# Attention and FFN layer in one kernel: values kept in SBUF, queries and keys projected from float32r halves, first maxima two halves at a time

## The chip, the cores and the metric

The kernel runs on one core of a Trainium2 chip. The metric is device time in microseconds of one execution, given as the median of several. The engines are TensorE (PE in the profile, its weight loads PEld), VectorE (DVE), ScalarE (ACT), GpSimd (POOL) and SyncE (SP), whose queue issues most DMAs. A name with a q behind it (SPq, ACTq) is an engine's sequencer.

## What is computed

One transformer layer on x of shape 8 x 1024 x 256, all in float32, for which the reference does

```python
q, k, v = (split_heads(x @ w.T * s + b) for each of q, k, v)     # 16 heads of 16
attn = softmax(q @ k.T / 4)                                      # 1024 x 1024 per head
x = layernorm(x + ((attn @ v) @ w_o.T * s_o + b_o))
gate, up = fp4(x) @ fp4(w_gate).T, fp4(x) @ fp4(w_up).T          # width 704, fp4 by blocks of 16
x = layernorm(x + fp4(silu(gate) * up) @ fp4(w_down).T)
```

The weights of q, k, v and o are whole multiples of 8 (0 and plus or minus 8).

## The kernel before

The program has three stages, each written as five programs (one for each engine) whose order is the order of the Python text. Nothing is reordered by a planner; the engines meet at semaphores.

**Stage 1, `project`** takes the 8192 tokens in 16 chunks of 512 (`C`). For a chunk, `transpose_x` (L397) turns x into PSUM banks 0 and 1, ACT copies it to `xT` (L466), and PE computes queries and keys (L437: four blocks `m` of 128 rows, each two float32 matmuls of 512 columns) and values (L447: four token tiles `j`, each two float32 matmuls of 256 columns). A float32 matmul stands in the trace as two records. ACT reads each block of queries or keys twice, as float32 (`qf`, L479) and rounded to float32r (`parts`, L482); DVE subtracts the one from the other (L517), so that a number is kept as the sum of two float32r halves. DVE also scales the values into `vaug` (L527), where a head takes 32 columns (`AV`), 16 of values and a one. SP stores the halves in `qk_dram` (L349) and the values in `v_dram` (L356).

From chunk 4 on (`MAX_FROM`) the row maxima of the first group of heads are taken beside this. `max_tile` (L416) makes the scores of 128 queries of one head with all 1024 keys, in two banks, and `take_max` (L503) reduces them to one maximum. There are 32 (`MU`) of these for a group of four heads, three to a chunk. PE may not write the two banks again before DVE has read them (`max_read`).

**Stage 2, `attend`** runs over 32 groups (8 batches x 4 groups of four heads). A group has 16 steps `s`, each of two half steps. In a half step PE computes two score tiles of the next step (L729) and, beside them in the other half of the array's rows, the two banks of one maximum of the group after (L709); then four matmuls, one for each head, which multiply 256 columns of the exponentials with `vs` (L757, eight records, 32 output rows per head, so the four stand side by side in the array). DVE reduces the maxima (L860), ACT takes the exponentials (L813). Maxima run four steps ahead (`AHEAD`): so the stage begins with steps 12 to 15 of a group -1, which hold eight maxima of group 1 and, at the end, the first scores of group 0. `load_stacks` (L580 to L591) loads queries, keys and values of group i + 2 into one of three slots (`RING`), at the start of group i. POOL meanwhile quantizes the FFN weights.

**Stage 3, `feed`**, runs over 64 tiles of 128 tokens and ends the kernel.

## Time and profile before

| | us |
|---|---|
| median of 3 runs | 2152.37 |
| lowest, highest | 2149.47, 2155.92 |
| the profiled execution | 2149.2 |
| span of its profile | 2147.0 |
| stage 1 (0 to 235), PE busy | 217 |
| stage 2 (235 to 1552), PE busy | 1288 |
| stage 3 (1552 to 2147), PE busy | 573 |

Times in rows are from the start of the span. PE busy is the union of matmul records, whose ends are modelled. "PEclk" is the TensorE clock that was granted, as a share of 2.4 GHz: 1.00 is 2.4 GHz and 0.50 is 1.2 GHz.

### The profile page before, as it was taken

What the parts mean: (1) busy time and instruction counts of PE and PEld (TensorE: products, weight loads), DVE (VectorE), ACT (ScalarE), POOL (GpSimd) and SP (SyncE); (2) the same over time, 40 slices, a digit from 0 to 9 for tenths busy, and PEclk for the clock granted to TensorE, in tenths of its full rate; (3) what the DMA queues carried; (4) which work ended last, traced back from release to release, by engine and by line L of the source; (5) the groups of instructions that cost most, each with busy time, mean ns of one, the idle gap of its engine ahead of it and who ended that gap; (6) DMA issues with size and microseconds to landing.
All of it is one profiled execution on the core that took longest, in us unless ns stands there. A gap on an engine that the chain in (4) does not pass through costs nothing.

```text
span 2147.0 us, 41870 instructions
## 1 busy us (share of the span) xinstructions
PE 2077.8 (97%) x15708; PEld 1062.5 (49%) x15708; DVE 1885.9 (88%) x2477; ACT 1658.9 (77%) x3230; POOL 800.2 (37%) x711
## 2 busy tenths in 40 slices
PE   7999999999999999999999999999979999999998
PEld 4455433333333333333333333333457777777776
DVE  3455799999999999999999999999079999999996
ACT  4445588888888888888888888888857777777775
POOL 3000399999200000000000000000058888888885
PEclk9999899999999999999999999999999999999999
DMA  7988833533533443443453353351121211111100
GB/s 234 300 265 244 238 57 57 89 59 52 91 62 52 78 75 52 73 76 56 68 79 57 64 85 56 56 82 27 46 76 58 63 60 60 62 60 60 60 31 21
DMA packets 171985, 184.48 MB, mean 86 GB/s; under 512 B 23622, under 2 KB 134598, under 8 KB 171782
## 3 DMA queue, kind: packets, MB, share of 16 engines
q1 hardware_dynamic: 164102, 174.19, 36.5%
q10 hardware_dynamic: 7392, 7.34, 1.1%
q8 instruction: 124, 2.03, 0.4%
q14 instruction: 79, 0.65, 0.1%
q0 software_dynamic: 288, 0.27, 0.1%
HBM read 104.14 MB, written 76.02 MB: 84 GB/s over the span
## 4 chain that ended last, share of the span: by engine, by line
PE 83%; DVE 10%; ACT 3%; DMA 2%; issue 1%; POOL 1%; SPq 0%; POOLq 0%; DVEq 0%; ACTq 0%
PE ps L709 25%; PE ps L757 24%; PE ps L1010 11%; DVE negmax L860 9%; PE ps L1032 8%; PE ps L437 5%; PE ps L999 2%; PE ps L447 2%; PE ps L1021 2%; ACT craw L821 2%; PE ps L729 2%; PE ps L1040 1%; PE ps L416 1%; DMA wgu<-in_L_ffn_w_up_dram 1%; PE ps L397 0%
## 5 line engine op out<-in xcount | busy, mean ns | idle before, releaser
L860 DVE TENSOR_REDUCE negmax<-ps 128x1 f32<-128x1024 f32 x992 | 1203.8, 1221 | 38.2 <-PE ps L709 28.4
L813 ACT ACTIVATE room<-ps 128x512 f32<-128x512 f32 x2048 | 1104.9, 598 | 168.0 <-PE ps L729 132.2
L729 PE MATMUL ps<-qs,ks 50*128 50x512 f32 x2048 | 754.6, 448 | 0.5 <-ACT room L813 0.5
L709 PE MATMUL ps<-ks,qs 48*128 48x512 f32 x1984 | 726.4, 446 | 19.4 <-DVE negmax L860 18.3
L757 PE MATMUL ps<-room,vs 128*32 128x256 f32 x8192 | 655.3, 392 | 9.3 <-ACT craw L821 0.2
L709 PEld LDWEIGHTS ps<-ks,qs 48*128 48x128 f32 x1984 | 293.8, 186 | 424.2 <-DVE negmax L860 316.0
L1255 POOL TENSOR_TENSOR ctxT<-cin 128x256 f32<-128x256 f32 x64 | 58.6, 915 | 996.7 <-DMA cin<-rden 996.7
L757 PEld LDWEIGHTS ps<-room,vs 128*32 128x32 f32 x8192 | 163.5, 108 | 376.7 <-issue 214.1
L729 PEld LDWEIGHTS ps<-qs,ks 50*128 50x128 f32 x2048 | 308.0, 185 | 17.3 <-ACT room L813 14.8
L1010 PE MATMUL ps<-wguT,xqT 128*128 128x512 f32 (+1 forms) x1152 | 264.9, 383 | 2.1 <-DVE xqT L1183 2.1
L1010 PEld LDWEIGHTS ps<-wguT,xqT 128*128 128x128 f32 x1152 | 209.2, 189 | 58.4 <-issue 20.2
L1032 PE MATMUL ps<-wdT,hT 128*128 128x256 f32 (+1 forms) x768 | 191.8, 392 | 3.9 <-ACT hT L1086 3.9
L1032 PEld LDWEIGHTS ps<-wdT,hT 128*128 128x128 f32 (+1 forms) x768 | 142.0, 192 | 43.7 <-issue 26.6
L899 POOL TENSOR_SCALAR fq<-fq 88x1024 f32<-88x1024 f32 (+1 forms) x42 | 137.4, 3271 | 3.6
L437 PE MATMUL ps<-xT,wT 128*128 128x512 f32 x256 | 123.0, 619 | 2.5 <-ACT parts L482 2.5
L1057 ACT ACTIVATE centre<-mv 128x1 f32<-128x1 f32 x128 | 25.6, 200 | 112.8 <-POOL rstd L1244 112.8
L1278 POOL TENSOR_TENSOR hg<-room,hm 128x704 f32<-128x704 f32 x64 | 97.4, 1522 | 9.4 <-DVE room L1164 8.4
L517 DVE TENSOR_TENSOR parts<-qf,parts 128x512 fp32r<-128x512 f32 x64 | 43.6, 687 | 56.4 <-ACT parts L482 56.4
L893 POOL TENSOR_TENSOR fq<-wgu,rcp_w 88x1024 f32<-88x1024 f32 x4 | 7.7, 1934 | 226.6 <-DMA v_ones<-vaug 226.3
L1283 POOL TENSOR_TENSOR hq<-hg,hs 128x704 f32<-128x704 f32 x64 | 88.7, 1386 | 5.5 <-PE ps L1021 0.5
L479 ACT ACTIVATE qf<-ps,b_col,s_all 128x512 f32<-128x512 f32 x64 | 49.7, 777 | 52.8 <-PE ps L437 46.1
L1157 DVE SCALAR_TENSOR_TENSOR room<-room,hs 128x704 f32<-128x704 f32 x64 | 86.8, 1355 | 0.1
(102 smaller groups left out, 2091.9 us busy)
## 6 DMA issues: line engine op xcount, KB each, us to landing
qk_parts<-parts SPq DMA_DIRECT2D x64, 512.0 KB, 5.1
qs<-qk_parts SPq DMA_DIRECT2D x192, 128.0 KB, 4.4
ks<-qk_parts SPq DMA_DIRECT2D x192, 128.0 KB, 7.1
v_ones<-vaug SPq DMA_DIRECT2D x64, 256.0 KB, 5.7
vs<-v_ones SPq DMA_DIRECT2D x32, 512.0 KB, 9.4
ctx_raw<-craw SPq DMA_DIRECT2D x64, 256.0 KB
cin<-ctx_raw SPq DMA_DIRECT2D x64, 128.0 KB
cin<-rden SPq DMA_DIRECT2D x64, 128.0 KB
```

Source lines behind the costliest of these rows:

```text
L437: last = nc.tensor.matmul(ps[:, QK + m % 2, :], wT[:, m // 2, c, (m % 2) * P:(m % 2 + 1) * P], xT[:, i.slot(2), c, :], start=c == 0, stop= ...
L709: return nc.tensor.matmul(ps[:, MX + 2 * (item[i.k, u] % 2) + bank, :], qs[rows, i.slot(RING), pair, t * P:(t + 1) * P], ks[rows, i.slot(R ...
L729: nc.tensor.matmul(ps[:, score_bank(i, s * GH + n), :], ks[rows, slot, pair, kt * P:(kt + 1) * P], qs[rows, slot, pair, qh * BANK:(qh + 1) ...
L757: last = nc.tensor.matmul(ps[h * AV:(h + 1) * AV, PV, cols], vs[:, i.slot(RING), kt, h * AV:(h + 1) * AV], prob[:, prob_slot(i, s), h, col ...
L813: nc.scalar.activation(prob[:, prob_slot(i, s), SCORE_ORDER[n], :], ps[:, score_bank(i, s * GH + n), :], ACT.Exp, scale=float(D) ** -0.5). ...
L860: nc.vector.tensor_reduce(negmax[:, j.slot(RING), max_column(u):max_column(u) + 1], ps[:, bank:bank + 2, :], AX.XY, ALU.max, negate=True). ...
L899: link(nc.gpsimd.tensor_scalar(dst, norm, mid * mid, gain, ALU.is_gt, ALU.mult))
L1010: last = nc.tensor.matmul(ps[:, GU + n0 // BANK, 0:n1 - n0], xqT[:, a, c, :], wguT[:, b, c, n0:n1], start=n == 0 and c == 0, stop=n == len ...
L1032: last = nc.tensor.matmul(ps[:, DN, 0:H], hT[0:rows, c, :], wdT[0:rows, c, :], start=c == 0, stop=c == IC - 1)
L1157: return nc.vector.scalar_tensor_tensor(out=by(self.norm), in0=by(self.src), scalar=NUDGE, in1=self.blocks[:, 2].unsqueeze(2).to_broadcast ...
L1278: nc.gpsimd.tensor_tensor(hg[:, :], hn[:, t.slot(2)], hm[:, t.slot(2)], ALU.subtract).then_inc(sems["hgrid_ready"], 1)
L1283: nc.gpsimd.tensor_tensor(hq[:, :].rearrange("p (n e) -> p n e", e=BLK), hg[:, :].rearrange("p (n e) -> p n e", e=BLK), hs[:, t.slot(2), 1 ...
```

## The change

**Stage 1.** Values stay in SBUF, in `vals` (64 token tiles x 16 heads x 17 columns, `DV` = 16 values and a one); `v_dram`, its 64 stores and the 32 loads into `vs` are gone. ACT copies x twice, as `xT` and rounded to float32r as `xh`; DVE makes the rest `xl` = xT - xh. Queries and keys are three products of halves (`PRODUCTS`), six float32r matmuls of 512 columns for each block instead of two float32 ones. The number of `qf` buffers goes from four to two. Maxima are taken in units of 128 queries of two heads, in the two halves of the array's rows, with 512 keys, four units to a chunk; a reduce gives two half maxima, which one `tensor_tensor` (`whole_max`) joins. Chunks 4 to 11 take the first group, chunks 12 and 13 the first eight units (`LEAD`) of group 1, so stage 2 begins at step 15 of group -1. At chunk 12 (`TURN`) the whole maxima of group 0 are formed and transposed. The scales of the FFN weights are computed in chunks 2, 3 and 14 from copies loaded into `stage`, no longer ahead of chunk 0; x of chunk 0 is loaded ahead of three of the four weights.

```diff
-        load_chunk(sp, At(None, 0, 2))
-        load_chunk(sp, At(None, 1, 2))
-        sp.wait_ge(qk_consts_in, 64)
-        for j in range(2):
-            sp.dma_start(wgu[:, j], ffn_ws[j]...).then_inc(ffn_w_in[j], 16)
-        sp.dma_start(wd[:, :, :], ffn_ws[2]...).then_inc(ffn_w_in[2], 16)
+        load_weights(0)
+        load_chunk(sp, At(None, 0, 2))
+        load_weights(1)
+        load_weights(2)
+        load_chunk(sp, At(None, 1, 2))
+        load_weights(3)
...
+        def queries_and_keys(i, m):
+            wait(pe, qk_float, i.lin(4, m - 1))
+            for n, (a, b) in enumerate(PRODUCTS):
+                if m == 0:
+                    pe.wait_ge(x_split if b else xh_ready, i.lin(1, 1))
+                x_half = xl if b else xh
+                for c in range(HC):
+                    last = nc.tensor.matmul(ps[:, QK + m % 2, :], wqk[:, a, m // 2, c, (m % 2) * P:(m % 2 + 1) * P],
+                                            x_half[:, i.slot(2), c, :], ...)
...
             wait(act, v_psum, i.lin(2, -2))
+            nc.scalar.activation(xh[:, i.slot(2)], ps[:, 0:2, :], ACT.Copy).then_inc(xh_ready, 1)
             nc.scalar.activation(xT[:, i.slot(2)], ps[:, 0:2, :], ACT.Copy).then_inc(xT_ready, 1)
...
-                wait(act, qk_split, i.lin(4, m - 3))
+                wait(act, qk_split, i.lin(4, m - 1))
...
         for i in chunks():
+            if i.plus(1).ok(NCH):
+                split_x(i.plus(1))
+            if i.k == TURN:
+                whole_max(0, S // P, MU)
+                maxima_out.split(nc, dve, ps[:, MX], At(None, 0, RING), first_maxima)
+            split_qk(i, 0)
+            take_max(i, 0)
+            split_qk(i, 1)
+            values(i, 0)
+            take_max(i, 1)
+            split_qk(i, 2)
+            take_max(i, 2)
+            split_qk(i, 3)
+            values(i, 1)
+            take_max(i, 3)
+            weight_scales(scale_job(i))
```

**Stage 2.** The values' matmuls read 17 columns of `vals` for a head and write 17 rows of PSUM, still from row 32 h on. The FFN weights are loaded here, ahead of the stacks of group 2.

```diff
-                last = nc.tensor.matmul(ps[h * AV:(h + 1) * AV, PV, cols],
-                                        vs[:, i.slot(RING), kt, h * AV:(h + 1) * AV],
+                last = nc.tensor.matmul(ps[h * AV:h * AV + DV, PV, cols],
+                                        vals[:, i.k // NG * KT + kt, i.k % NG * GH + h, :],
...
-            for s in range(ST - AHEAD if i.k < 0 else 0, ST):
+            for s in range(ST - 1 if i.k < 0 else 0, ST):
...
     def sync(sp):
-        pass_1_stored(sp)
+        projections_done(sp)
+        for j in range(2):
+            sp.dma_start(wgu[:, j], ffn_ws[j]...).then_inc(ffn_w_in[j], 16)
+        sp.dma_start(wd[:, :, :], ffn_ws[2]...).then_inc(ffn_w_in[2], 16)
```

Stage 3 does the same work; its buffers, and the memory of `cin`, `xin3`, `wguT` and `wdT`, now lie where `vals` lies, and SP has one more wait (`pv_done` of group 28) ahead of the first loads of the last stage.

On PE a chunk with maxima stood so before (`xT`, `xin` are x, `ps` is PSUM):

```order
L397 MATMUL ps<-ident,xin 128x128 x8
L437 MATMUL ps<-xT,wT 128x512 x2
L416 MATMUL ps<-ks,qs 128x512 x2
L437 MATMUL ps<-xT,wT 128x512 x4
L416 MATMUL ps<-ks,qs 128x512 x2
L437 MATMUL ps<-xT,wT 128x512 x2
L447 MATMUL ps<-wT,xT 128x256 x4
L416 MATMUL ps<-ks,qs 128x512 x2
L447 MATMUL ps<-wT,xT 128x256 x4
```

and the first half of one stands so now (the `qs` read by L478 is where `xh` lies, L465 are the maxima, L488 the values):

```order
L437 MATMUL ps<-ident,xin 128x128 x8
L478 MATMUL ps<-qs,wqk 128x512 x2
L478 MATMUL ps<-xl,wqk 128x512 x2
L478 MATMUL ps<-qs,wqk 128x512 x2
L465 MATMUL ps<-ks,qs 128x512 x2
L488 MATMUL ps<-wT,xT 128x256 x2
L478 MATMUL ps<-qs,wqk 128x512 x2
L478 MATMUL ps<-xl,wqk 128x512 x2
L478 MATMUL ps<-qs,wqk 128x512 x2
L488 MATMUL ps<-wT,xT 128x256 x2
L465 MATMUL ps<-ks,qs 128x512 x2
```

Three visits to the maxima have become four, and values and queries alternate. On PE the end of stage 1 and the start of stage 2 stood so before:

```order
L447 MATMUL ps<-wT,xT 128x256 x8
L709 MATMUL ps<-ks,qs 128x512 x13
L729 MATMUL ps<-qs,ks 128x512
L709 MATMUL ps<-ks,qs 128x512
L729 MATMUL ps<-qs,ks 128x512
L709 MATMUL ps<-ks,qs 128x512
```

and stand so now:

```order
L488 MATMUL ps<-wT,xT 128x256 x2
L835 MATMUL ps<-qs,ks 128x512 x4
L815 MATMUL ps<-ks,qs 128x512
L835 MATMUL ps<-qs,ks 128x512
L815 MATMUL ps<-ks,qs 128x512
L835 MATMUL ps<-qs,ks 128x512
```

The sixteen matmuls of eight maxima (L709) ahead of and beside the first scores (L729) are gone; four scores (L835) stand alone, and then the steps of group 0 begin. On SP, stage 2 begins now with

```order
L392 DMA qk_parts<-parts 128x2x512 [waits qk_split] x8
L765 DMA wgu<-in_L_ffn_w_gate_dram 88x8x256 [waits v_ready,qk_stored1,qk_stored0]
L765 DMA wgu<-in_L_ffn_w_up_dram 88x8x256
L766 DMA wd<-in_L_ffn_w_down_dram 128x2x704
L691 DMA qs<-qk_parts 16x2x1024 x6
L691 DMA ks<-qk_parts 16x2x1024 x6
```

so three loads of 704 KB stand in the queue ahead of the twelve of group 2.

## Rows read from the trace of the kernel before

**Rows 1.** Windows: us, busy us (instructions) of each engine, PEclk, DMA share, GB/s.

```profile
0.00:235.00 235.00, 216.91 (x721) 122.07 (x721) 116.09 (x171) 112.39 (x149) 19.72 (x21) 0.98 0.89 270
249.00:1552.00 1303.00, 1277.31 (x12223) 482.06 (x12215) 1217.98 (x1075) 1130.91 (x2102) 292.53 (x118) 1.00 0.38 65
239.00:256.00 17.00, 16.34 (x70) 6.04 (x68) 13.54 (x12) 8.71 (x16) 8.56 (x4) 0.50 0.91 206
```

**Rows 2.** Chain of waits through one chunk: start us, us, what.

```profile
100.76 0.87 PE ps L397 x8
101.64 1.72 PE ps L437 x4
103.36 0.66 PE ps L416 x2
...
108.31 1.91 PE ps L437 x4
110.22 1.73 PE ps L447 x8
```

**Rows 3.** Chain of waits at the start, before chunk 1.

```profile
12.71 12.96 DMA wgu<-in_L_ffn_w_up_dram
...
31.59 0.64 DVE parts L517
```

**Rows 4.** Timeline: the wait for group 0's stacks at chunk 4.

```profile
73.19 1.22 PE L416 MATMUL ps<-ks,qs 48*128 48x512 f32 x2 [5.27 <-DMA vs<-v_ones]
74.34 5.78 PE L437 MATMUL ps<-xT,wT 128*128 128x512 f32 x8
```

**Rows 5.** Groups by line, 87 to 222 us: busy us, mean ns, idle before.

```profile
L503 DVE TENSOR_REDUCE negmax<-ps 128x1 f32<-128x1024 f32 x29 | 35.5, 1225 | 27.7 <-PE ps L416 27.7
L479 ACT ACTIVATE qf<-ps,b_col,s_all 128x512 f32<-128x512 f32 x40 | 31.1, 777 | 28.4 <-PE ps L437 28.4
...
L517 DVE TENSOR_TENSOR parts<-qf,parts 128x512 fp32r<-128x512 f32 x40 | 27.5, 687 | 31.4 <-ACT parts L482 31.4
...
L527 DVE SCALAR_TENSOR_TENSOR vaug<-ps,s_all,b_row 128x256 f32<-128x256 f32 x39 | 16.2, 478 | 0.0
...
L466 ACT ACTIVATE xT<-ps 128x1024 f32<-128x1024 f32 x10 | 10.2, 1023 | 41.2 <-PE ps L397 41.2
```

**Rows 6.** DMA issues of the start: KB each, median us to landing.

```profile
xin<-in_L_attn_x_dram SPq DMA_DIRECT2D x2, 512.0 KB, 10.0
```

**Rows 7.** Timeline from stage 1 into stage 2: start us, us, instruction, [idle before].

```profile
235.52 0.74 PE L709 MATMUL ps<-ks,qs 48*128 48x512 f32 x4 [1.17 <-DVE vaug L527]
...
238.53 2.37 DVE L860 TENSOR_REDUCE negmax<-ps 128x1 f32<-128x1024 f32 x2
...
248.56 1.08 PE L757 MATMUL ps<-room,vs 128*32 128x256 f32 x8
...
256.71 0.64 PE L757 MATMUL ps<-room,vs 128*32 128x256 f32 x8
```

**Rows 8.** Timeline of PE in the middle of stage 2.

```profile
1000.24 0.49 PE L709 MATMUL ps<-ks,qs 48*128 48x512 f32 x1
...
1000.90 0.64 PE L757 MATMUL ps<-room,vs 128*32 128x256 f32 x8
...
1001.47 0.49 PE L709 MATMUL ps<-ks,qs 48*128 48x512 f32 x1
```

**Rows 9.** Groups by form, 257 to 1552 us, weight loads: mean ns.

```profile
L709 PEld LDWEIGHTS ps<-ks,qs 48*128 48x128 f32 x1954 | 287.6, 184 | 411.7 <-DVE negmax L860 308.3 <-issue 103.4
L757 PEld LDWEIGHTS ps<-room,vs 128*32 128x32 f32 x8152 | 162.6, 107 | 373.8 <-issue 211.8 <-ACT room L813 161.3
```

**Rows 10.** Chain of waits in stage 3: float32r matmuls of 512 and 384 columns.

```profile
1709.88 4.06 PE ps L1010 x18
```

**Rows 11.** Chain of waits, half steps at the two levels of the clock.

```profile
255.11 1.01 PE ps L757 x8
...
256.78 0.57 PE ps L757 x8
```

More of the change, by code:

```diff
@@ L240, in build @@
+        third = feed(nc, sb, sem, room, buffers, x_tok, ctx_dram, rden_dram, out_tok, ps, ident, wT, s_all, b_row,
+                     wguT, wdT, wt_ready, wt_split, numbers, sums, craw_stored, rden_ready, rden_stored, cin, xin,
+                     c_in, x_in)
         with nc.Block() as block:
@@ L308, in max_tiles, with unit_at, scale_job, staged @@
         first = (i.k - MAX_FROM) * MAX_PER
-        return range(first, min(first + MAX_PER, MU))
+        return range(first, min(first + MAX_PER, MU + LEAD))
+    def unit_at(u):
+        group, n = divmod(u, MU)
+        return group, n // (2 * GP), (n // 2) % GP, n % 2
+    def scale_job(i):
+        return {MAX_FROM - 2: 0, MAX_FROM - 1: 1, NCH - 2: 2}.get(i.k)
+    def staged(job):
+        if job == 2:
+            return stage[:, 0:HC * I]
+        return stage[0:I // 8, :]
     def chunks():
@@ L421, in tensor, with values @@
+        def values(i, j):
+            if j % 2 == 0:
+                wait(pe, v_ready, i.lin(2, j // 2 - 1))
+            for c in range(HC):
+                last = nc.tensor.matmul(ps[:, VV + j // 2, (j % 2) * H:(j % 2 + 1) * H],
+                                        xT[:, i.slot(2), c, j * P:(j + 1) * P], wT[:, 0, c, :],
+                                        start=c == 0, stop=c == HC - 1)
+            if j % 2 == 1:
+                last.then_inc(v_psum, 1)
         for i in chunks():
@@ new lines, in take_max, with whole_max @@
+                nc.vector.tensor_reduce(both[:, :, pair * (S // P) + t:pair * (S // P) + t + 1], ps[:, MX:MX + 2, :],
+                                        AX.X, ALU.max, negate=True).then_inc(max_read, 1)
+        def whole_max(group, tiles, done):
+            whole, first, second = (a.rearrange("p (h t) -> p h t", t=S // P)[:, :, 0:tiles]
+                                    for a in (negmax[:, group], halfmax[:, group, 0], halfmax[:, group, 1]))
+            dve.wait_ge(max_read, done)
+            nc.vector.tensor_tensor(whole, first, second, ALU.min).then_inc(max_whole, 1)
@@ L642, in items @@
         for g in range(1, NGR):
[L643 removed]
+            for u in range(LEAD if g == 1 else 0, MU):
                 yield g, u
```

364 lines of the change are left out of this document (199 added, 165 removed).

## The prediction

> **What bounds the kernel now.** I read the windows by stage first [rows 1]. Stage 1 takes 235 us with PE busy for 217 of them and DMA at 0.89; stage 2 takes the most, PE busy 98% of it, DVE 93%. The chain of waits says which of these ends last. In a chunk of stage 1 it runs through PE alone, piece on piece [rows 2]: 0.87 for the transposes, 1.72 for four records of queries or keys, 0.66 for a visit to the maxima. A visit also makes the next four records 1.91 instead of 1.72, so it costs 0.66 + 0.19 = 0.85. A chunk is 0.87 + 4 x 1.72 + 2 x 1.73 + 3 x 0.85 = 13.8 us with maxima and 11.2 without. DVE is idle 27.7 us behind PE's maxima and 31.4 behind ACT [rows 5], so it has room here.
>
> In stage 2 the reader is to see that DVE is not the bound, though it is 93% busy. A half step is 1.23 us, from one L709 to the next [rows 8], and no idle time stands before the second on PE. Two reduces back to back take 2.37 [rows 7], so one every 1.14. PE is full: float32r matmuls for 0.66, values for 0.57 [rows 8, 11]. Whatever shortens PE's half step counts 1024 times, until about 1.14.
>
> **The change, part by part.** The sum is made against the profiled execution, 2149.2 us, which is 3.2 below the median.
>
> (1) The start of stage 1. Before, DVE waited for the FFN weights and computed their scales, and its first subtraction came at 31.59 [rows 3]. That goes. What is late next is the last of the 2 MB of w and x: its second x chunk landed about 10 us after issue at 2.7 [rows 6], and as much is loaded now. With the transposes of w_o and the copy behind it (about 1.5), chunk 0 begins at 14.5.
>
> (2) A chunk on PE. Transposes 0.87. Queries and keys: 24 float32r matmuls of 512 columns. Eighteen of the same form, 8448 columns, took 4.06 [rows 10], so one of 512 takes 0.246 and 24 take 5.9, where 16 records took 6.9. The bounds are the columns alone at 2.4 GHz (0.213, 5.1) and the 0.33 of one in a visit, where its weight load is not hidden [rows 2] (7.9). I take 5.9, the nearest form. Values stay at 3.46. A visit still has two matmuls, but in different rows of the array, as L709 and L729 have in stage 2, where they start together; 0.21 of columns goes from 0.85, so 0.64 (bounds 0.43 and 0.85). A chunk without maxima is 10.2 and one with four visits 12.8.
>
> The Trainium skill ("TensorEngine Tiling (Array Packing)", Key Properties) says that a change of tiling mode, not of tile, drains the array. By that the two halves share one drain, and the visit is 0.64; if a change of tile drained too, it would be 0.85, 40 times, 8.4 us more.
>
> (3) ACT and DVE in a chunk. ACT gets a second copy of 1.02 and has eight of 0.78, about 8 us with its DMA issue: still under PE. DVE has four reduces (4.6 at 1.14 each; two outputs instead of one, same input, so I keep 1.14 and allow 1.3), four subtractions 2.5, values 1.7 and the new subtraction on 1024 columns, about twice 0.69 less its fixed part, 1.2 (bounds 0.69 and 1.37). That is 10, beside 12.8 on PE [rows 5, 7]. But there is one pair of banks for the maxima, so PE waits where a reduce is late. Walking one chunk through the order of the three engines: the copies end 3.3 after the chunk's start, the new subtraction at 4.5, the first reduce starts at 5.5 and ends at 6.7, while PE is at the second unit at 6.25. Such waits come to 0.9. So 13.7 for a chunk with maxima.
>
> (4) Single waits in stage 1. Group 0's stacks are loaded in chunk 2 and wanted in chunk 4, as before; then PE waited 5.3 us [rows 4]. Chunk 3 is 1 us shorter now, the thirteenth load (vs) is gone: I take 4.4, between 0 and 7. Behind that wait PE ran at half pace, L416 1.22 for two [rows 4] instead of 0.66 and the eight records of L437 after it 5.8 instead of 3.6; the same loss again, 2.7. At chunk 12 the whole maxima wait behind x of chunk 13 on DVE (transposes, two copies, subtraction), and PE waits for them: 4.0. The scales of chunks 2, 3 and 14 lie in DVE's idle time, and SP's wait for them holds back stores that nobody waits for. Group 1's stacks, loaded in chunk 4, are wanted eight chunks later.
>
> Sum: 14.5 + 6 x 10.2 + 10 x 13.7 - 0.9 (the last chunk transposes nothing) + 4.4 + 2.7 + 4.0 = 222.9, against 234.35, where PE's last values ended, 235.52 less 1.17 [rows 7]. **Gain 11.5**, between -3 and 22.
>
> (5) The start of stage 2. From 234.35 to the first values at 248.56 [rows 7] was 14.2 us, with eight reduces in it. Those reduces are in chunks 12 and 13 now, paid in (2). What is left: DVE's last subtraction and values 2.2, four scores of which the fourth waits for the first exponential 1.6, two half steps that exponentials pace 2.3, 0.7 of the third: 6.8. Before, PE idled and its clock was at 1.2 GHz from 239 to 256 [rows 1, 7], and the four half steps from 248.56 to 256.71 took 8.15 instead of 4.9. PE now works up to the change of stage, but idles 2.2 and is half empty for 4 us, so I allow 1.4 for a short fall of the clock. **Gain 14.2 - 8.2 = 6**, and 2.5 of the 3.2 of the slow half steps.
>
> (6) The values' weights. A load of 128 columns takes 184 ns and one of 32 takes 107 [rows 9], 0.8 ns for a column, so 17 should take 94 or 95. Of the eight loads of a half step four lie under matmuls and four, side by side, are exposed, since they follow matmuls of another shape. Eight records took 0.57 [rows 11] where two passes of 256 float32 columns are 0.43; at 1.2 GHz they took 1.01, with the passes alone 0.85. So part of the 0.14 is the columns of those loads, once. 15 columns fewer at 0.8 ns is 12.5 ns, times 1024: **gain 12.8**. The bounds: 0, if the array loads 32 columns anyway, and 12.8; nothing shows more.
>
> "TensorE: Matmul & The Clock Gate" of the Trainium skill (LDWEIGHTS) has the load as columns over 1.2 GHz, with no step at 32; the slope between the two rows agrees, and no run here shows 17.
>
> (7) Hidden. The 16.8 MB of values written and as much read (of 184) leave DMA, which bounds no stage. FFN loads of 2.1 MB at 200 to 300 GB/s, about 10 us, and stacks behind them: they land some 25 us after stage 2 begins, wanted at step 12 of group 0, about 31 us in. POOL starts quantizing as late as before and has 1300 us. SP's wait for group 28 is met by the wait ahead of it. Stage 3 has the same work. All nothing; if the stacks came late, a few us once.
>
> Sum: 11.5 + 6 + 2.5 + 12.8 = 32.8. 2149.2 - 32.8 = 2116.4; on the median **2119**.
>
> **The rivals.**
> - A: 17 columns load like 32. Neither row speaks for it; nothing below 32 is in the trace. 2119 + 13 = 2132.
> - B: DVE and PE catch each other more often in a chunk (two outputs slow the reduce, a reduce of 1.3 four times, and drains between value and query matmuls): 14.7 instead of 13.7, 2129. For it: the one pair of banks. Against: DVE's 10 of 13.7.
> - C: a float32r matmul in stage 1 takes the 0.33 of a visit. 24 x 0.085 x 16 = 33 us, the gain is gone: 2152. Against it stand the eighteen of rows 10, also on changing weights.
> - D, the other side: PE's waits in chunks 4 to 13 let the clock fall, as at 239, and it stays there: at 1.2 GHz it was busy 16.3 of 17 us and still not raised [rows 1]. A chunk's 12.8 of PE work would be 25.6, ten times: +120, 2239. It decides once more than 79 us are at half clock, each costing half (32.8 + 6.5). Against: those waits are 7% of a chunk, and the clock was 0.98 over a stage 1 that had longer ones [rows 1, 4].
> - E: with 17 rows per head the four value matmuls no longer run side by side. That is the change not doing what it says: over 1000 us more. Against it: each head still starts at its own row 32 h.
>
> **How the numbers follow.** Forecast 54%, A 26%, B 9%, C 4%, D 3%, E 2%, other ways to a gain under 0.3% 2%. 0.3%, 6.5 us, is what a measurement of this kernel can tell from no change. Faster: 54 + 26 + 9 = 89%; same: 4 + 2 = 6%; slower: 5%. The range goes from 2106 (the stage 1 terms at their good ends, no fall of the clock) to 2138, which takes in A and B.
>
> **What would show it.** PEld of the 17-column load at 94 ns and half steps of 1.218 (A: 107 and 1.230). Chunks 14.7 us or less apart, the eighteen-like pitch of 0.24 for L478 (C: 0.33). The last L488 near 223, the first L863 near 231. PE clock 1.00 in chunks 5 to 11 (D). I would be wrong in kind if half steps grew longer or if stage 3 moved by more than 3 us.

## The result, and the profile after

| | before | changed |
|---|---|---|
| median of the runs | 2151.7 | 2131.3 |
| the profiled execution | 2149.2 | 2129.3 |
| span of its profile | 2147.0 | 2127.5 |

The ratio is 0.990, with a 95% interval of 0.988 to 0.992: about 1% faster, where 2119 was forecast. In a later set, beside other runs of the kernel before, the changed kernel gave 0.986 (0.983 to 0.989), 2126.6 us. So the gain is 20 to 30 us by the medians, and 19.5 between the two profiled spans. The working below is made against the spans. One of the four executions of the changed kernel took 2230.7 us at a mean granted clock of 0.84, where the others had 0.99; it is left out of the ratio, and as it has no trace, where its clock was low is not known.

The windows of the changed kernel by stretch (us, then busy us and instructions of each engine, granted clock, DMA share, GB/s):

```profile
58.00:85.00 27.00, 16.42 (x55) 11.16 (x53) 12.18 (x15) 7.81 (x11) 0.00 (x0) 0.75 0.71 215
85.00:216.00 131.00, 119.51 (x533) 84.28 (x532) 95.87 (x126) 72.39 (x96) 0.00 (x0) 0.99 0.63 196
216.00:240.00 24.00, 21.14 (x92) 15.38 (x90) 14.18 (x23) 15.18 (x24) 0.00 (x0) 0.84 0.65 220
240.00:1530.00 1290.00, 1264.04 (x12172) 455.47 (x12171) 1211.99 (x1074) 1129.87 (x2099) 294.38 (x118) 1.00 0.32 55
```

Read against [rows 1]: stage 2 is PE's as before, and DMA carries less. One stretch stands out, 58 to 85 us: PE is busy 16.4 of 27 us and its clock is 0.75. That is chunk 4.

A steady chunk with maxima, on PE's timeline. The reader is to see the transposes at 98.42 and the next ones at 111.84:

```profile
98.42 1.09 PE L437 MATMUL ps<-ident,xin 128*128 128x128 f32 x8
99.27 0.71 PE L478 MATMUL ps<-qs,wqk 128*128 128x512 f32 x2
99.82 0.62 PE L478 MATMUL ps<-xl,wqk 128*128 128x512 f32 x2
100.29 0.63 PE L478 MATMUL ps<-qs,wqk 128*128 128x512 f32 x2
...
101.38 0.49 PE L465 MATMUL ps<-ks,qs 48*128 48x512 f32 x2 [0.47 <-DVE halfmax L561]
...
111.84 1.09 PE L437 MATMUL ps<-ident,xin 128*128 128x128 f32 x8
```

A chunk takes 13.42 us (forecast 13.7). Two float32r matmuls of the queries (99.82) start 0.47 before the next two (100.29), so one takes 0.23. Without maxima a chunk is 9.88 (forecast 10.2): the transposes start at 28.04, 37.92, 47.80 and 57.68.

Chunk 4, all engines together:

```profile
56.08 0.38 SPq L381 DMA_DIRECT2D stage<-in_L_ffn_w_up_dram  x1
...
64.41 0.50 PE L465 MATMUL ps<-ks,qs 48*128 48x512 f32 x2 [4.31 <-DMA ks<-qk_parts]
...
69.72 2.28 DVE L595 TENSOR_REDUCE amax_w<-stage 88x128 f32<-88x2048 f32 x1 [9.74 <-DMA stage<-in_L_ffn_w_up_dram]
...
74.84 1.22 DVE L561 TENSOR_REDUCE halfmax<-ps 128x2 f32<-128x1024 f32 x1
...
76.11 0.80 PE L465 MATMUL ps<-ks,qs 48*128 48x512 f32 x2 [6.27 <-DVE halfmax L561]
...
85.02 1.09 PE L437 MATMUL ps<-ident,xin 128*128 128x128 f32 x8
```

It took 85.02 - 57.68 = 27.3 us, where 20.8 was forecast. The wait for the stacks is there, 4.31 us, as forecast. The second wait was not in the sum. The up weights for the scales were asked for at 56.08, behind the twelve loads of the stacks. DVE came to them at 60 and stood 9.74 us. Behind that wait, in DVE's order, lay the subtraction on x, a subtraction for the queries and the first maxima of chunk 4, which came at 74.84 though its matmuls stood ready at 64.9. PE had nowhere to put the second unit until then. In the seven profiles, this one and six below, that leave the loads of chunks 2 to 4 as they are here, chunk 4 takes 26.3 to 27.9 us.

The change of stage, on PE's timeline:

```profile
232.65 1.19 PE L835 MATMUL ps<-qs,ks 50*128 50x512 f32 x3 [2.39 <-DVE vals L606]
...
238.21 1.05 PE L863 MATMUL ps<-room,vals 128*17 128x256 f32 x8
...
248.89 0.87 PE L863 MATMUL ps<-room,vals 128*17 128x256 f32 x8
...
250.35 0.63 PE L863 MATMUL ps<-room,vals 128*17 128x256 f32 x8
```

PE's last values of stage 1 end at 232.65 - 2.39 = 230.3. The first values of stage 2 follow 7.9 us later (8.2 forecast). Then six half steps take 250.35 - 238.21 = 12.14 us where six of 1.22 are 7.3: the clock was at 1.2 GHz, and 4.8 us went there.

The middle of stage 2, PE's timeline, and the weight loads by form (busy us, mean ns), to be held beside [rows 8, 9]:

```profile
1000.11 0.49 PE L835 MATMUL ps<-qs,ks 50*128 50x512 f32 x1
...
1001.33 0.49 PE L835 MATMUL ps<-qs,ks 50*128 50x512 f32 x1
```

```profile
L815 PEld LDWEIGHTS ps<-ks,qs 48*128 48x128 f32 x1968 | 291.6, 185 | 428.1 <-DVE negmax L968 316.0 <-issue 112.0
...
L863 PEld LDWEIGHTS ps<-room,vals 128*17 128x17 f32 x8192 | 138.1, 95 | 378.5 <-issue 216.3 <-ACT room L919 161.4
```

A load of 17 columns takes 95 ns (107 before), and a half step 1.22 instead of 1.23.

Stage 2 ends with the last copy of ACT, here in the changed kernel, and below it in the kernel before:

```profile
1532.88 0.60 ACT L927 ACTIVATE craw<-ps 128x512 f32<-128x512 f32 x1 [1.46 <-PE ps L863]
```

```profile
1552.42 0.60 ACT L821 ACTIVATE craw<-ps 128x512 f32<-128x512 f32 x1 [1.48 <-PE ps L757]
```

From the first values to the end of that copy: 1533.48 - 238.21 = 1295.3, before 1553.02 - 248.56 = 1304.5. Behind it both have 594.0 us to their ends.

### The profile page after: what moved, and what is told of

It is laid out like the page before. It is cut to its first block, busy times and chain, and to the rows that moved or that the text cites. A ratio compares the mean times of both kernels' runs of the same rounds, so it can differ in the third digit from the quotient of the medians.

```text
span 2127.5 us, 42069 instructions
## 1 busy us (share of the span) xinstructions
PE 2044.5 (96%) x15836; PEld 1061.2 (50%) x15836; DVE 1900.4 (89%) x2497; ACT 1672.7 (79%) x3246; POOL 800.2 (38%) x712
## 4 chain that ended last, share of the span: by engine, by line
PE 77%; DVE 10%; ACT 3%; issue 1%; POOL 0%; POOLq 0%; DVEq 0%
PE ps L815 25%; PE ps L863 23%; PE ps L1128 12%; DVE negmax L968 9%; PE ps L1150 8%; PE ps L1117 3%; PE ps L1139 2%; ACT craw L927 2%; PE ps L835 2%; PE ps L1158 1%; PE ps L478 1%; PE ps L488 0%; DVE halfmax L561 0%; DVE vals L606 0%; ACT parts L550 0%
## 5 line engine op out<-in xcount | busy, mean ns | idle before, releaser
L968 DVE TENSOR_REDUCE negmax<-ps 128x1 f32<-128x1024 f32 x984 | 1189.3, 1221 | 36.4 <-PE ps L815 30.8
L835 PE MATMUL ps<-qs,ks 50*128 50x512 f32 x2048 | 756.7, 450 | 3.1 <-DVE vals L606 2.4
L863 PE MATMUL ps<-room,vals 128*17 128x256 f32 x8192 | 642.9, 386 | 9.2 <-ACT craw L927 0.2
L863 PEld LDWEIGHTS ps<-room,vals 128*17 128x17 f32 x8192 | 138.1, 95 | 378.5 <-issue 216.3
L835 PEld LDWEIGHTS ps<-qs,ks 50*128 50x128 f32 x2048 | 308.2, 185 | 22.4 <-ACT room L919 16.2
L1150 PEld LDWEIGHTS ps<-wdT,hT 128*128 128x128 f32 (+1 forms) x768 | 141.2, 191 | 43.1 <-issue 26.3
L478 PE MATMUL ps<-qs,wqk 128*128 128x512 f32 x256 | 91.9, 441 | 0.0
```

What stands on the lines that cost most here:

```text
L478: last = nc.tensor.matmul(ps[:, QK + m % 2, :], wqk[:, a, m // 2, c, (m % 2) * P:(m % 2 + 1) * P], x_half[:, i.slot(2), c, :], start=n == ...
L835: nc.tensor.matmul(ps[:, score_bank(i, s * GH + n), :], ks[rows, slot, pair, kt * P:(kt + 1) * P], qs[rows, slot, pair, qh * BANK:(qh + 1) ...
L863: last = nc.tensor.matmul(ps[h * AV:h * AV + DV, PV, cols], vals[:, i.k // NG * KT + kt, i.k % NG * GH + h, :], prob[:, prob_slot(i, s), h ...
L968: nc.vector.tensor_reduce(negmax[:, j.slot(RING), max_column(u):max_column(u) + 1], ps[:, bank:bank + 2, :], AX.XY, ALU.max, negate=True). ...
L1150: last = nc.tensor.matmul(ps[:, DN, 0:H], hT[0:rows, c, :], wdT[0:rows, c, :], start=c == 0, stop=c == IC - 1)
```

## Where the 19.5 us come from

| | forecast | measured, and how |
|---|---|---|
| stage 1 on PE | 11.5 | 4.1: 234.35 before [rows 7], 230.26 now |
| change of stage | 6 | 6.3: 14.2 before, 7.9 now |
| slow half steps | +2.5 | -1.6: they cost 3.2 before [rows 7], 4.8 now |
| 17 columns | 12.8 | 10.8: stage 2 without its slow half steps, 1304.5 - 3.2 before, 1295.3 - 4.8 now |
| stage 3 | 0 | 0.0 |
| sum | 32.8 | 19.5 (19.6 by the rounded terms) |

Three terms fell short: stage 1, the slow half steps and the 17 columns. The experiments ask what the stall of chunk 4 consists of, whether the column width is what shortened stage 2, and what holds the clock down at the change of stage. Each ratio below is against runs of the kernel before made beside that kernel (their medians are 2153.7 to 2157.8). The changed kernel's own ratio came out at 0.990 and 0.986, so a difference of a few us between kernels is read from their traces, not from their medians.

## Experiments on stage 1

**The up weights' scales at chunk 7 instead of 3.**

```diff
-        return {MAX_FROM - 2: 0, MAX_FROM - 1: 1, NCH - 2: 2}.get(i.k)
+        return {MAX_FROM - 2: 0, MAX_FROM + 3: 1, NCH - 2: 2}.get(i.k)
```

> The changed kernel, with one thing moved: the scales of the up weights (their load on SP and their three instructions on DVE) come at chunk 7 instead of chunk 3. My theory: the long chunk 4 of the changed kernel (27.3 us between its transposes and those of chunk 5, against about 20.8 in my forecast) comes from DVE, which stood 9.74 us at the end of chunk 3 waiting for that load, because the load was issued behind the twelve loads of the stacks; everything queued on DVE behind it came late, and PE waited 6.27 us for a maximum. By that the wait disappears and chunk 4 takes 20 to 21.5 us, the half-clock stretch from 71.9 to 82.2 shrinks, and the time falls by 5 to 8 us against the changed kernel, to about 2124.5 (ratio to the kernel before 0.987). Rival: chunk 4 is long because the stacks land late (PE's own wait of 4.31 us for ks) and the clock is low afterwards, DVE being late only in the shade of that; then chunk 4 stays above 25 us and the time within 2 us of 2131. Second rival: the wait moves with the load to chunk 7 and costs the same there.

2123.9 us, ratio 0.986 (0.984 to 0.987). PE's timeline in chunk 4 and chunk 8:

```profile
65.84 0.80 PE L465 MATMUL ps<-ks,qs 48*128 48x512 f32 x2 [6.27 <-DMA ks<-qk_parts]
75.05 0.49 PE L465 MATMUL ps<-ks,qs 48*128 48x512 f32 x2 [0.43 <-DVE halfmax L561]
...
127.78 0.49 PE L465 MATMUL ps<-ks,qs 48*128 48x512 f32 x2 [2.43 <-DVE halfmax L561]
```

And DVE's, for the job of chunk 7 (PE is in chunk 8 by then):

```profile
121.40 2.27 DVE L595 TENSOR_REDUCE amax_w<-stage 88x128 f32<-88x2048 f32 x1
123.71 0.22 DVE L598 TENSOR_SCALAR amax_w<-amax_w 88x128 f32<-88x128 f32 x1
123.97 0.95 DVE L601 RECIPROCAL rcp_w<-amax_w 88x128 f32<-88x128 f32 x1
```

The wait for a maximum went from 6.27 to 0.43 and chunk 4 from 27.3 to 21.2 us, all as the theory has it: DVE's stall was its own cost and lay in no shade. The wait for ks stayed, and is 6.27 now, since the stacks are late by themselves. But the three instructions are not free elsewhere: chunk 8 took 17.0 instead of 13.4, because in a chunk with maxima DVE's 3.4 us stand in front of the next subtraction and the next maximum. PE waited 2.43 us there, and the clock was at 1.2 GHz from 128.4 to 131.8 behind it. The second rival was right about the place, though not about the mechanism: the load had landed, DVE's own work was the cost.

**Group 0's stacks a chunk earlier.**

```diff
-            group = {MAX_FROM - 2: 0, MAX_FROM: 1}.get(i.k)
+            group = {MAX_FROM - 3: 0, MAX_FROM: 1}.get(i.k)
```

> The changed kernel with the loads of group 0's stacks one chunk earlier: SP issues them behind the stores of chunk 1 instead of behind those of chunk 2. They are then ahead of both loads of weights for the scales. Theory: PE's wait of 4.31 us for ks in chunk 4 goes (they land about 10 us earlier), and DVE's wait of 9.74 us for the up weights at the end of chunk 3 goes too, since nothing large is queued ahead of that load any more; chunk 4 takes 13.5 to 15 us instead of 27.3, with the clock at full speed. That is 12 to 13 us: 2118 to 2119, ratio 0.9815. Rival: the gate weights' load is now the one that queues behind the stacks, and DVE stands for it at the end of chunk 2 as long as it stood before at chunk 3; the stall moves from chunk 4 to chunk 3, and only PE's 4.3 and the low clock behind it are saved: 5 to 7 us, about 2125.

2135.7 us, 0.991 (0.989 to 0.992): chunk 4 grew to 32.1. The theory fell. The rival had the queue right, but not the size. DVE's timeline:

```profile
64.93 2.28 DVE L595 TENSOR_REDUCE amax_w<-stage 88x128 f32<-88x2048 f32 x1 [14.42 <-DMA stage<-in_L_ffn_w_gate_dram]
```

Now the gate weights queue behind the stacks, and DVE stands 14.4 us for them instead of 9.7. The stacks themselves had landed at 60.5 instead of 64.4. But ACT, with two `qf` buffers, stood 15.8 us behind DVE's late subtractions, and PE stood 12.6 us from 59.1 on; whether the four buffers of before would have held this off was not tested. What counts is not how early the stacks are, but which load is asked for behind them and who stands in line for it.

The Trainium skill ("DMA: Bandwidth & Descriptors", Queues, rings and completion order) gives SP one ring on each DMA engine, whose descriptors are taken in the order of the ring, though a later DMA may still complete first. The rows of the two kernels agree with the order: up was asked for at 56.08 behind the stacks and was there at 69.72; in the other kernel gate stood in that place, asked for at 50.8 and there at 64.9.

**The whole maxima of group 0 ahead of the subtraction in chunk 12** (DVE).

```diff
+            if i.k == TURN:
+                whole_max(0, S // P, MU)
             if i.plus(1).ok(NCH):
                 split_x(i.plus(1))
             if i.k == TURN:
-                whole_max(0, S // P, MU)
                 maxima_out.split(nc, dve, ps[:, MX], At(None, 0, RING), first_maxima)
```

> The changed kernel, and on DVE in chunk 12 the whole maxima of group 0 come ahead of the subtraction on the next chunk's x instead of behind it. In the changed kernel PE waits there 3.82 us (for DVE, which waits for ACT's two copies), its clock then is at half from 184.6 to 188.0, and chunk 12 takes 18.6 us where its neighbours take 13.4. Theory: the wait falls to under 1 us, and the clock stays up: chunk 12 takes 14.0 to 14.8, 4 us less, time about 2127. Rival: PE's wait only moves, since the split of the transposed maxima on DVE is still behind the subtraction, and PE's maxima of group 1 wait for that: 1 us less at most, within 1.5 us of 2131.

2125.0 us, 0.986 (0.983 to 0.988). PE's wait before, and with the edit:

```profile
183.81 0.28 PE L149 MATMUL ps<-ident,negmax 128*32 128x128 f32 x1 [3.82 <-DVE negmax L570]
```

```profile
182.28 0.28 PE L149 MATMUL ps<-ident,negmax 128*32 128x128 f32 x1 [2.09 <-DVE negmax L570]
```

Chunk 12 takes 15.9 us instead of 18.6, and the clock did not fall behind it. That is 2.7 of the 4 us expected, and more than the 1 us that the rival allowed: what stays of the wait is the last maximum of chunk 11, which DVE has still to take. The same wait of 2.1 us in the last kernel below did have a fall of the clock behind it, and chunk 12 took 16.9 there; so a us of this gain can come and go.

**All three moved: scales at chunks 0 and 1, stacks at 1, whole maxima first.**

```diff
-        return {MAX_FROM - 2: 0, MAX_FROM - 1: 1, NCH - 2: 2}.get(i.k)
+        return {0: 0, 1: 1, NCH - 2: 2}.get(i.k)
...
-            group = {MAX_FROM - 2: 0, MAX_FROM: 1}.get(i.k)
+            group = {MAX_FROM - 3: 0, MAX_FROM: 1}.get(i.k)
```

(and the edit of chunk 12 above)

> The changed kernel with three moves: the scales of the gate and up weights at chunks 0 and 1 (loads ahead of the stacks, and in chunks without maxima, since at chunk 7 the three instructions cost PE 3.6 us), the stacks of group 0 loaded behind chunk 1's stores, and the whole maxima ahead of the subtraction in chunk 12. Theory: chunk 4 takes 13.5 to 14.5 us instead of 27.3, chunk 12 14.0 to 14.8 instead of 18.6, all others as they were: 17 us less, 2114, ratio 0.982. Since the clock never falls between 21 and 230 us, this also tests that its falls in chunks 4 and 12 are only consequences of the waits. Rival: the steady chunks hide a limit that the stalls let recover (DMA of the stores, or ACT), so that chunks 5 to 11 grow to 14 or more; or the gate load, now right behind the first weights, delays the start of chunk 0 by 1 to 3 us; then 2117 to 2120.

2121.3 us, 0.983 (0.981 to 0.986), 7 short of the theory. Chunks 5 to 11 stayed at 13.4 and chunk 0 began at 15.0, so both rivals fell. Chunk 4 still took 23.9. The timelines of ACT and PE, and the window in which SP asks for the stacks:

```profile
68.35 0.78 ACT L547 ACTIVATE qf<-ps,b_col,s_all 128x512 f32<-128x512 f32 x1 [8.64 <-DMA qk_parts<-parts]
```

```profile
61.31 0.50 PE L465 MATMUL ps<-ks,qs 48*128 48x512 f32 x2 [2.62 <-DMA ks<-qk_parts]
71.71 0.79 PE L465 MATMUL ps<-ks,qs 48*128 48x512 f32 x2 [4.97 <-DVE halfmax L561]
```

```profile
46.00:57.00 11.00, 11.00 (x58) 9.38 (x57) 6.49 (x11) 9.21 (x13) 0.00 (x0) 1.00 0.96 158
```

DVE no longer waits for weights. But chunk 2's stores of q and k now lie behind the stacks, and ACT may not write chunk 4's halves over them until they have landed: 8.64 us. It is the same stall with a third engine in it. The DMA share is 0.96 in that window, at 158 GB/s.

**All scales late, at chunks 13, 14 and 15.**

```diff
-        return {MAX_FROM - 2: 0, MAX_FROM - 1: 1, NCH - 2: 2}.get(i.k)
+        return {NCH - 3: 0, NCH - 2: 1, NCH - 1: 2}.get(i.k)
```

> The changed kernel with all three jobs of scales late: gate, up and down weights at chunks 13, 14 and 15, so that no weights for scales (1.4 MB) are loaded before chunk 4. With the stall of DVE taken away, chunk 4 still took 21.2 us (up at chunk 7) or 23.9 (stacks earlier as well, where ACT then waited 8.6 us for stores of q and k), and DMA is over 95% busy from 30 to 65 us in all of them. Theory: what is left of the stall in chunk 4 is a backlog of DMA: stores, x, stacks and scale weights together need longer than four chunks of 9.9 us, and who waits is only a matter of order. By that 0.7 MB less ahead of the stacks (the gate weights, 3 to 4 us at 200 GB/s) brings ks 3 to 4 us earlier and chunk 4 to 17 to 18.5 us; with PE's rate elsewhere unchanged 9 us less than the changed kernel, 2120 to 2122. Rival: the stacks are late because SP issues them late, behind stores whose data come late from DVE, and each takes its 7 to 10 us whatever the load; then chunk 4 stays at 21 us and the time at 2124 to 2125. Second rival: the scales at chunks 13 to 15 cost PE or the first maxima of stage 2 what they save, 2 us each.

2121.2 us, 0.983 (0.979 to 0.986), 5.4 below the changed kernel on the same chip. Chunk 4: 19.4. PE's wait, and windows of this kernel and of the changed one:

```profile
65.49 0.79 PE L465 MATMUL ps<-ks,qs 48*128 48x512 f32 x2 [4.55 <-DMA ks<-qk_parts]
```

```profile
30.00:65.00 35.00, 30.93 (x150) 25.82 (x148) 19.80 (x32) 25.96 (x34) 0.00 (x0) 0.97 0.84 244
```

```profile
30.00:65.00 35.00, 30.69 (x150) 25.45 (x149) 20.07 (x31) 25.50 (x34) 0.00 (x0) 1.00 0.93 267
```

The time was as expected, chunk 4 was not (17 to 18.5), and the reason fell. With 1.4 MB less in the stretch, 0.7 of it ahead of the stacks, DMA is at 0.84 instead of 0.93. But PE's wait for ks is 4.55 us here, and in the seven profiles that leave those loads as the changed kernel has them it is 3.8 to 6.1; in the first experiment it was 6.27. So the loads' bytes cannot be seen in that wait, and what this kernel gains is DVE's stall and no more. What is left speaks for the rival. SP asks for the stacks from 50.7 to 57.5, behind chunk 2's last stores, and ks lands 8 us after the last of them, as it did in the changed kernel (asked for by 56.0, there at 64.4). Which part of those 8 us is the load on DMA and which a transfer's own time was not separated. The second rival was true in part: DVE stood 1.5 us for its weights in chunk 14, PE waited 3.5 us for the last values instead of 2.4, and from the last values of stage 1 to the first of stage 2 it took 9.1 us instead of 7.9.

**Filling matmuls at the start of stage 1** (eight on the identity ahead of each weight's transposes).

```diff
+        fill_start(8)
         weights_by_input(0)
...
         for m in range(1, 4):
+            fill_start(8)
             weights_by_input(m)
```

> The changed kernel with 32 matmuls more at the start of stage 1 (128x128, float32, on the identity, read by nobody), eight ahead of the transposes of each weight, where PE waits for DMA 2 to 4 us each time. In the changed kernel PE's clock is at half until 20.7 us and chunk 0 takes 12.3 us instead of 9.9. Theory: low activity keeps the clock down; with the waits filled it rises before chunk 0 begins and chunk 0 takes 9.9 to 10.5: 1.5 to 2.4 us less (2129). Rival: the clock is low in the first 20 us whatever PE does; then chunk 0 stays at 12.3 and the fillers, at half clock 1.9 us for eight, push the start of chunk 0 by up to 2 us: 2131 to 2133.

2125.7 us, 0.985 (0.983 to 0.988). PE's timeline:

```profile
1.52 3.48 PE L443 MATMUL ps<-ident 128*128 128x128 f32 x16 [1.52 <-POOL ident L399]
...
17.60 1.09 PE L437 MATMUL ps<-ident,xin 128*128 128x128 f32 x8 [0.69 <-ACT wT L536]
...
27.54 1.04 PE L437 MATMUL ps<-ident,xin 128*128 128x128 f32 x8
```

Both sides came true. Eight transposes take 1.09 us at 17.60, where those at 15.76 in the changed kernel take 1.97, and chunk 0 took 9.9 us instead of 12.3, and instead of the 11.3 to 12.8 of the other changed kernels: the pace there is a matter of PE's work. It is read from these durations, since the profile's own row of the granted clock says 1.00 for the changed kernel's first 20 us. But the fillers made chunk 0 start 1.8 us later, and chunk 1 began at 27.54 instead of 28.04; in the kernels without them it began anywhere from 26.5 to 28.9, so nothing is shown to be won.

## Experiments on stage 2 and the change of stage

**32 columns again.** Each head's 17 columns and the 15 behind them.

```diff
-                last = nc.tensor.matmul(ps[h * AV:h * AV + DV, PV, cols],
-                                        vals[:, i.k // NG * KT + kt, i.k % NG * GH + h, :],
+                at = ((i.k // NG * KT + kt) * NH + i.k % NG * GH + h) * DV
+                last = nc.tensor.matmul(ps[h * AV:(h + 1) * AV, PV, cols],
+                                        vals[:, at:at + AV],
```

(`vals` is passed as one flat row here, with 15 more columns at its end)

> The changed kernel, with the values' weights read 32 columns wide again: each head's 17 columns and the 15 that follow them in the same tile, into 32 rows of the bank, of which the upper 15 are read by nobody. Vals stays 17 columns per head in memory. My theory: the 17-column load is what shortened the half step in stage 2, so the load is 107 ns again, the half step 1.230 instead of 1.218, and stage 2 is 12 us longer: 2143 to 2144, ratio to the kernel before about 0.996. Rival: the half step got shorter for another reason (less DMA traffic, no stack of values to read), and the load's width is hidden: then the time stays within 2 us of the changed kernel's 2131.

2142.1 us, 0.994 (0.993 to 0.996). Its weight loads, PE's timeline at the change of stage, and ACT's last copy:

```profile
L867 PEld LDWEIGHTS ps<-room,vals 128*32 128x32 f32 x8192 | 163.8, 108 | 378.8 <-issue 217.9 <-ACT room L923 160.3
```

```profile
235.63 1.08 PE L867 MATMUL ps<-room,vals 128*32 128x256 f32 x8
...
261.06 0.64 PE L867 MATMUL ps<-room,vals 128*32 128x256 f32 x8
```

```profile
1546.86 0.60 ACT L931 ACTIVATE craw<-ps 128x512 f32<-128x512 f32 x1 [1.48 <-PE ps L867]
```

The load is at 108 ns again. Stage 2 takes 1547.46 - 235.63 = 1311.8 us, of which 10.7 are slow half steps: twelve took 25.43 instead of 12 x 1.23. Without them it is 1301.1, and the kernel before has 1304.5 - 3.2 = 1301.3. With 17 columns it is 1290.5 in the changed kernel and, with no slow half step to take off, 1290.5 in the last kernel below. So the width is the whole gain of stage 2, 10.6 us by this kernel and 10.8 by the one before; the traffic of the values that stay on chip is worth nothing there. The edit widens the load and the rows that the matmuls write together, so that it is the load of the two is read from its 95 and 108 ns.

**Ten filling matmuls at the change of stage**, where PE waits 2.39 us.

```diff
+        def fill(bank, n):
+            for _ in range(n):
+                nc.tensor.matmul(ps[:, bank, :], qs[0:KR, 0, 0, 0:P], ks[0:KR, 0, 0, 0:BANK], start=True, stop=True)
         pe.wait_ge(first_maxima, 1)
+        fill(MX, 10)
         pe.wait_ge(qk_float, 4 * (T // BANK))
```

> The changed kernel with ten matmuls more on PE (48 rows, 128x512, float32r, their result read by nobody) at the change from stage 1 to stage 2, where PE waits 2.39 us for DVE's last values. The granted clock falls to half (1.2 GHz) at 232.4 us and comes back at 249.4, and six half steps take 2.136 us instead of 1.218. Theory: the clock falls because PE idles 2.4 us there; the ten matmuls fill that idle time (2.3 us at 0.23 each), nobody waits for them, and the half steps from 238 on take 1.22: 4 to 7 us less, 2124 to 2127. Rival: what lowers the clock is the stretch behind it, where the first scores wait for the first exponentials and PE is half empty for 5 us; then the fall only comes some us later, the slow half steps stay five or six, and the time is within 1.5 us of 2131 (or 1 us above it, if the ten delay the first scores).

2128.9 us, 0.988 (0.987 to 0.990). The windows:

```profile
232.00:237.00 5.00, 4.55 (x21) 2.55 (x21) 2.76 (x6) 3.16 (x7) 0.00 (x0) 1.00 0.48 157
237.00:248.00 11.00, 11.00 (x64) 3.46 (x64) 6.92 (x6) 6.22 (x12) 0.00 (x0) 0.53 1.00 167
```

The rival held in its mechanism: the fall came 5 us later, and four and a half half steps were slow, one less than before. The only gap of PE in that stretch was 0.45 us, at 234.0, where the first scores wait for an exponential.

**Eight more, between the first scores.**

```diff
                 max_and_scores(j, u, ahead, 0)
+                if 16 * i.k + s <= 0:
+                    fill(PV, 2)
```

(and the same behind the second pair of scores)

> The kernel with ten idle-time matmuls at the change of stage, and eight more of the same form in the stretch behind it: two after each pair of scores of the first two steps of stage 2, where PE waits for ACT's exponentials, written into the bank of the values before its first use. With the ten alone the clock fell at 237.3 instead of 232.4 and was back at 247.5, and 4.6 half steps were slow instead of 5.4. Theory: the clock falls for want of PE work in the 5 us of the first scores; with the stretch filled it stays at full speed, all half steps are 1.22, and the time is 4 us below the kernel with ten alone, about 2125. Rival: the clock falls at that place whatever PE does, since the load on the chip rises when the full rate of stage 2 begins; then five half steps are slow again and the time is 2129 or, with the eight in the way of the scores, 2130.

2123.8 us, 0.984 (0.982 to 0.987). The window:

```profile
229.00:240.00 11.00, 10.81 (x74) 6.24 (x72) 7.04 (x9) 8.49 (x17) 0.00 (x0) 1.00 0.66 189
```

PE is busy 10.8 of 11 us, the clock stays at 1.00, no half step is slow, and the eight do not delay the scores. The rival, that the clock falls there whatever PE does, is out for this kernel.

**Late scales, whole maxima first and the fillers together.**

```diff
+        return {NCH - 3: 0, NCH - 2: 1, NCH - 1: 2}.get(i.k)
...
+        fill(MX, 10)
```

> The changed kernel with three things that each helped alone or should: scales at chunks 13 to 15, the whole maxima of group 0 ahead of the subtraction in chunk 12 (it took 15.9 us instead of 18.6), and the eighteen filling matmuls at the change of stage (no slow half step instead of five, and the clock at full speed from 188 us on). Theory: the gains lie at different places and add up: 9 to 10 in chunk 4, 2.7 in chunk 12, 5 to 6 at the change of stage, so 17 to 18 us below the changed kernel, 2113, ratio to the kernel before 0.981. Rival: what is gained in stage 1 is given back at the change of stage, where the first half steps then meet the FFN weights' load and the stacks of groups 1 and 2; then 2118 or more.

2119.3 us, 0.981 (0.979 to 0.984): 7 below the changed kernel on the same chip, not 17 to 18. PE's timeline and the window:

```profile
222.38 0.47 PE L836 MATMUL ps<-qs,ks 50*128 50x512 f32 x1 [0.74 <-issue]
```

```profile
223.00:240.00 17.00, 16.86 (x98) 7.75 (x99) 11.61 (x13) 10.85 (x21) 0.00 (x0) 0.60 0.90 198
```

Stage 1 gave what it should: PE's last values end at 219.1 instead of 230.3. Part was given back, as the rival says, though not to the loads it named. The scales in chunk 14 had to wait 1.4 us for their weights and made DVE's last values late; the ten fillers ran out, PE stood 0.74 us, and the clock fell at 223.2. Four half steps were slow and the first values came 10.2 us after the last ones of stage 1, instead of 7.9.

**The changed kernel again**, beside the kernel with late scales and the one with all of them together.

> The changed kernel itself, unchanged, beside the other two, so that their differences are read on one chip. Expected by all theories: 2127 to 2132 and a ratio of 0.986 to 0.990 to the kernel before. How long the clock stays at half after the change of stage (17 us in the first profile, 10 to 20 in kernels that did not touch that place) is expected to differ again: if it does, that length is no effect of the edits.

2126.6 us (2124.9 to 2133.1), 0.986 (0.983 to 0.989). Its profiled execution is the longest of the six:

```profile
232.00:257.00 25.00, 23.01 (x120) 8.54 (x120) 14.21 (x15) 13.87 (x26) 2.28 (x2) 0.52 0.86 162
```

The clock was at half for 24 us, and eight half steps and part of a ninth were slow, where the first profile had five and part of a sixth. So the length of this stretch differs from one execution to the next, by some 3 us of time, and no edit is to be credited with it.

**A version faster than all of these.** Scales at 0, 13 and 15; twelve fillers and the eight; whole maxima first.

```diff
+        return {0: 0, NCH - 3: 1, NCH - 1: 2}.get(i.k)
...
+        fill(MX, 12)
```

> The kernel with late scales, whole maxima first and the filling matmuls, with two repairs at the change of stage: the scales come at chunks 0 (its load behind the first weights, where DMA has room), 13 and 15, so that none stands on DVE in chunk 14, where DVE waited 1.43 us for the load and made the last values late; and twelve filling matmuls at the change of stage instead of ten. In that kernel PE had 0.74 us of idle time behind the ten, the clock fell at 223.2 and four half steps were slow; in the kernel with fills alone PE had no idle time there and no half step was slow. Theory: what keeps the clock up at the change of stage is that PE stays without a gap; with none left, no half step is slow, the first values follow the last values of stage 1 after 7 us instead of 10.2, and the time is 2112 to 2114, 5 us below that kernel. Rival: the earlier result was chance, the clock falls at this place in most executions; then there are four or more slow half steps again and the time is 2116 to 2119. In stage 1 chunk 4 is expected at 18 to 19.5 us and chunk 12 at 15.9 as before, since DMA has the same bytes to move ahead of it, less at the busy time.

2112.2 us (2111.7 to 2115.0), 0.979 (0.977 to 0.981). The window and ACT's last copy:

```profile
216.00:240.00 24.00, 23.99 (x183) 13.02 (x183) 20.48 (x24) 18.62 (x34) 0.00 (x0) 1.00 0.88 204
```

```profile
1517.42 0.60 ACT L937 ACTIVATE craw<-ps 128x512 f32<-128x512 f32 x1 [1.46 <-PE ps L864]
```

PE is without a gap through the change of stage, the clock is at 1.00, and no half step is slow. The first values come 7.1 us after the last ones of stage 1, at 227.57, and stage 2 takes 1290.45. Chunk 4 was 19.2 and chunk 12 16.9 (15.9 expected), with the clock at 1.2 GHz from 174.1 to 177.5. Which of the two repairs closed the gap of 0.74 us was not separated. The eleven profiles of the changed kernel and its variants with a gap or a half-empty stretch there all have slow half steps, two to twelve; the two without have none. The executions without a trace lean the same way: their mean granted clocks are 0.990 to 0.996 in these two kernels, and 0.987 to 0.992 in the later set of the changed one. That the fillers prevent the fall is shown; how large a gap it takes is not.

## Why the prediction was right, and where it was not

- **The size.** 2131.3 lies in the range of 2106 to 2138 and the direction is right; the forecast of 2119 was 12 us too good. 13.3 of the 32.8 us did not come.
- **(1)** Chunk 0 began at 15.8, not 14.5, and took 12.3 instead of 10.2, since PE's matmuls ran at half pace until about 20.7 (two of L478 took 1.05 us, then 0.62): 3.4 us in all. 2.1 of them are the pace, since I had costed the start by its transfers alone. The rest is a misreading of [rows 6]: the 10.0 there is the median of two x chunks, and in the trace of before the first, asked for at 2.74, landed at 11.9 and the second, asked for at 3.25, at 14.1. The last weights landed at 13.9 now, not at 13.
- **(2), (3)** Held: 0.23 for a matmul (0.246), 9.88 for a chunk (10.2), 13.42 with maxima (13.7). PE waits 0.85 us in such a chunk (0.9), which leaves (13.42 - 9.88 - 0.85) / 4 = 0.67 for each of its four visits (0.64, and not the 0.85 of a second drain). That is 3.5 us better over the thirteen chunks that had no single wait. DVE's sum was 0.4 too low by its own rows: four subtractions at 0.687 are 2.7 and not 2.5, four values at 0.478 are 1.9 and not 1.7; nothing hung on it. Rivals B and C fell.
- **(4)** This is the step that failed: "The scales of chunks 2, 3 and 14 lie in DVE's idle time, and SP's wait for them holds back stores that nobody waits for." I weighed DVE's work against its idle time and did not ask when its input lands. The load stood behind twelve others on SP, DVE stood for it, and a subtraction and a maximum that PE needs stood behind DVE. Chunk 4 cost 27.3 and not 20.8, 6.5 us; the first experiment took 6.1 of them away with that one wait. Nor is the work itself free in a chunk with maxima: at chunk 7, with its load long there, it cost PE 3.6 us. Chunk 12 was 0.9 over its term.
- **(5)** The step from stage to stage held, 6.3 for 6. "I allow 1.4 for a short fall of the clock" did not: the fall was as long as before, 17 us, and took in six half steps instead of four, 4.1 us short of the term. I took PE to be warm because it worked up to the change; the 2.4 us without work and the half-empty stretch behind it were enough. With both filled, the fall was gone.
- **(6)** The mechanism was right, and the 32-column kernel shows that it is all of stage 2's gain. The size was 10.8 and not 12.8. Half of a us of that is in the sum itself, where 15 columns at 0.8 ns were put at 12.5 ns and are 12.0; the load did get 12 ns shorter, on the line through the two rows. The rest is that not every half step gained: of each 32 half steps, counted from the first of stage 2, most got 9 to 17 ns shorter, but the first and the 17th (1.31 us before and after) and the 23rd (2.00) did not. Rival A fell.
- **(7)** FFN loads, POOL, the stacks of later groups and stage 3 cost nothing, as said; stage 3 is 594.0 in both.
- **D** fell as a catastrophe in every profile: the clock came back within chunk 4 and was 0.99 from 85 to 216. In small it was true, in chunks 4 and 12 and at the change of stage.
- **E** fell: the eight records of a half step's values take 0.63 us, before 0.64.

## What to carry to other kernels

When work is moved into another engine's idle time, check three things and not one: its duration, when its input lands given what is queued ahead of it on the same issuing engine, and what stands behind it in the moved-to engine's order. A stall made of a full queue moves on when one of its waits is removed, here from DVE to ACT; moving a load out of the stretch did more (chunk 4 at 18.4 to 19.4 us with the scales' loads elsewhere) than asking for the stacks earlier (32.1, and 23.9 with the scales moved too). Where a pipeline changes over, ask for gaps on TensorE: twenty matmuls whose result nobody reads, put into waits that were there anyway, took away half steps at half clock that cost 2 to 11 us in the other kernels.

## What the hardware showed that was not expected

- A gap of 0.74 us on PE, ahead of a stretch that exponentials pace, was followed by a clock at 1.2 GHz, and it came back only at 237 though PE's records fill 16.9 of the 17 us from 223. Before, 16.3 of 17 us had not raised it either [rows 1]. With ten fillers alone the only gap ahead of the fall was 0.45 us. Yet in chunks 5 to 11 PE waits 0.4 to 0.5 us twice in each, and the clock stays at 1.00 there; so the length of the gap alone does not tell. The Trainium skill ("TensorE: Matmul & The Clock Gate", HAM oscillation) describes falls behind waits for DMA. The trace agrees in chunk 4: the clock fell at 65.1 behind the wait of 4.31 us for ks. It fell again at 71.9, in a wait of 6.27 us for DVE. That gaps as short as 0.74 and 0.45 us can stand before a fall, only the runs show.
- The busy share of DMA does not tell what is moved. In the changed kernel it was 1.04 at 314 GB/s from 50 to 57 us, while SP asked for the stacks, and in the kernel with three things moved 0.96 at 158 GB/s from 46 to 57, where SP asked for them too. Why is open.
- Two executions of the same program differed in how long the clock stayed at half at the same place, 17 and 24 us.
